# In the last expert slot, the loads of Q, K and V wait block by block for the stores that they read

## What is computed

```python
logits = xn @ sn - sigmoid(gates)            # 4096 x 16 experts
w = softmax over the active experts          # at least two of them
y = einsum('nc,ech->neh', x, p)              # p: q_proj, k_proj, v_proj
q, k, v = einsum('ne,neh->nh', w, y)         # each 4096 x 128
attn = softmax(q @ k.T / sqrt(128))          # all 4096 keys for all queries
o = attn @ v
out = einsum('enh,ehc->nc', w * o, o_proj)   # 16 experts back to 256 channels
return x + gb * out
```

## Time and profile before

| | us |
|---|---|
| median of 3 runs (1463.3 to 1464.61) | 1464.16 |
| profiled execution | 1462.89 |
| its span, first to last instruction | 1461.2 |
| PE busy | 1378.4 (94%) |
| DVE busy | 1157.5 (79%) |
| POOL busy | 710.0 (49%) |
| ACT busy | 672.8 (46%) |

### The profile page before, as it was taken

One profiled execution on the slowest core, in us unless ns is written; L12 is line 12 of the kernel. 1 busy time (PEld: TensorE's weight loads), 2 busy tenths in 40 slices (PEclk: granted clock), 3 DMA queues, 4 the chain that ended last, 5 costly groups with the idle time before them and its releaser, 6 DMA issues. The chain is left out here.

```text
span 1461.2 us, 20840 instructions
## 1 busy us (share of the span) xinstructions
PE 1378.4 (94%) x6884; PEld 1210.1 (83%) x6884; DVE 1157.5 (79%) x2192; ACT 672.8 (46%) x1331; POOL 710.0 (49%) x628
## 2 busy tenths in 40 slices
PE   5578999999999999999997989999999999999998
PEld 3458989999999999999997966878788787878776
DVE  5758586785876868767665888999999999989876
ACT  3340221302213022130011079888888888888983
POOL 3221131301313113121013167888889888988897
PEclk9688999999999999999999999999999999999999
DMA  4230110011100111000106450000000000000000
GB/s 135 72 97 15 31 38 27 26 39 31 38 27 26 38 31 38 27 26 24 52 25 209 148 192 15 8 23 21 15 30 15 30 16 29 15 22 16 15 15 30
DMA packets 84668, 63.24 MB, mean 43 GB/s; under 512 B 15520, under 2 KB 77392, under 8 KB 84304
## 3 DMA queue, kind: packets, MB, share of 16 engines
q1 hardware_dynamic: 56656, 46.69, 10.2%
q10 hardware_dynamic: 27904, 15.21, 3.5%
HBM read 36.72 MB, written 25.17 MB: 42 GB/s over the span
## 5 line engine op out<-in xcount | busy, mean ns | idle before, releaser
L1473 PE MATMUL ps<-w_hi,memory_r 128*128 128x384 f32 x2048 | 569.7, 343 | 5.8 <-DVE w_lo L886 3.0
L1246 DVE SCALAR_TENSOR_TENSOR wst<-ps,w_cur,wst 128x384 f32<-128x384 f32 x480 | 295.4, 615 | 171.1 <-PE ps L1473 157.8
L1473 PEld LDWEIGHTS ps<-w_hi,memory_r 128*128 128x128 f32 x2048 | 376.8, 189 | 10.0 <-DVE w_lo L886 3.1
L1690 POOL TENSOR_TENSOR memory_rest<-memory_rest,pf 128x512 f32<-128x512 f32 x248 | 346.4, 1397 | 67.0 <-ACT pf L1797 58.4
L1473 PE MATMUL ps<-w_lo,memory_r 128*128 128x384 f32 x1024 | 344.9, 337 | 0.0
L1863 DVE TENSOR_TENSOR p_lo<-pf,p_hi 128x512 fp32r<-128x512 f32 x256 | 282.4, 1103 | 34.3 <-ACT p_hi L1799 33.3
L1473 PEld LDWEIGHTS ps<-w_lo,memory_r 128*128 128x128 f32 x1024 | 194.3, 190 | 4.8 <-issue 1.4
L1797 ACT ACTIVATE pf<-ps 128x512 f32<-128x512 f32 x256 | 153.1, 598 | 71.7 <-PE ps L1969 54.7
L1757 ACT COPY ps<-shift_rows 128x512 f32<-128x512 f32 x254 | 151.7, 597 | 5.9
L1799 ACT ACTIVATE p_hi<-ps 128x512 fp32r<-128x512 f32 x256 | 152.0, 594 | 0.0
L1844 DVE TENSOR_REDUCE mx<-ps 128x1 f32<-128x512 f32 x224 | 147.7, 679 | 1.2 <-PE ps L1958 1.2
(11 more groups left out here) (216 smaller groups left out, 2105.0 us busy)
## 6 DMA issues: line engine op xcount, KB each, us to landing
qk_scratch<-wst ACTq DMA_DIRECT2D x56, 128.0 KB, 2.2
memory<-in_x SPq DMA_DIRECT2D x8, 512.0 KB, 4.0
x_scratch<-memory SPq DMA_DIRECT2D x8, 512.0 KB, 2.9
o_scratch<-memory_rest SPq DMA_DIRECT2D x16, 256.0 KB, 3.1
x2b<-x_scratch SPq DMA_DIRECT2D x32, 128.0 KB, 2.2
out_x<-memory_rest SPq DMA_DIRECT2D x32, 128.0 KB, 1.7
v_scratch<-wst ACTq DMA_DIRECT2D x60, 64.0 KB, 1.8
memory_r<-qk_scratch SPq DMA_DIRECT2D x9, 256.0 KB, 4.5
```

The lines of the kernel that those rows point to most:

```text
L1246: nc.vector.scalar_tensor_tensor(out=dst, in0=src, scalar=w, in1=dst, op0=ALU.mult, op1=ALU.add).then_inc(moe_acc, 1)
L1473: ins = nc.tensor.matmul(ps[:, s % MOE_BANKS, 0:H3], x_part[p][:, k, rows], w_part[:, k, e].rearrange("p t h -> p (t h)"), start=(k == 0 a ...
L1690: nc.gpsimd.tensor_tensor(p_sum[:, p], p_sum[:, p], pf[:, j % PB], ALU.add).then_inc(p_summed, 1)
```

## The change

The two waits for the stores of all 28 tiles of blocks 0 to 6 go. Ahead of the queries stands a wait for the stores of eight tiles, that is blocks 0 and 1. Ahead of each high key block g stands a wait for the Q and K stores of tiles up to the end of block g, and ahead of the low keys and values of block g one for the V stores up to there. No instruction is moved from its place in any queue, and the other engines' programs are the same.

```diff
                         sp.wait_ge(moe_mm, (NB - 1) * STEPS)
                         sp.wait_ge(u_ready, NB)
                         sp.wait_ge(bu_mm, NB)
-                        sp.wait_ge(qk_out, 32 * (NT - TT))
-                        sp.wait_ge(v_out, 32 * (NT - TT))
+                        sp.wait_ge(qk_out, 32 * 2 * TT)
 
                         def load_queries(n):
                             for l, q_part in enumerate((q_hi, q_lo)):
@@ -507,11 +506,13 @@
                         def load_high_keys(g0, g1):
                             for g in range(g0, g1):
                                 keys = slice(g * BT, (g + 1) * BT)
+                                sp.wait_ge(qk_out, 32 * (g + 1) * TT)
                                 sp.dma_start(k_hi[:, keys].bitcast(F32), qk_dram[0, :, 1, keys]).then_inc(k_in[g], 16)
 
                         def load_rest(g0, g1):
                             for g in range(g0, g1):
                                 keys = slice(g * BT, (g + 1) * BT)
+                                sp.wait_ge(v_out, 32 * (g + 1) * TT)
                                 sp.dma_start(k_lo[:, keys].bitcast(F32), qk_dram[1, :, 1, keys]).then_inc(kv_in[g], 16)
```

## The result

The changed kernel took 1452.29 us, the median of four runs (1451.81 to 1453.87), against 1464.38 us for the kernel before in the same comparison. The ratio is 0.9922, with a 95% interval of 0.991 to 0.9935. The profiled execution took 1451.81 us, 11.1 us less than that of before, and its span is shorter by 11.1 us too.

What follows compares the result with a forecast made beforehand. TensorE, 94% busy, was taken as the bound, with time to gain where it stalls or runs at a lower clock. Median 1464.16 less 10.63 us for the stall gave 1453.5 us; range 1451.8 to 1456.8.

Steps and rivals of the forecast that it cites:

- The wait that goes: SP queue, last expert slot: 11.3 + 1.2 us of waiting ahead of the first load goes; load issued at about 757.3.
- rival E: SP queue: another wait, hidden behind line 499, ends as late, so no gain: 1464.2 us, chance 0.02.
- The met waits: SP's added waits for stores long landed: 0.05 us each, 0.2 us for four among the first keys.
- The arrival of the keys: Key block 0 lands at 763.1, 3.3 us before PE needs it at 766.45 for the first maximum.
- The cost of the stall: PE at the first maximum in the last slot: 10.63 us lost, 9.06 waiting and about 1.57 lower clock and restart.
- The output chain: Output-part stores behind the loads: first group ends near 783, second starts at 787.9, an estimated 3 us late, covered; cost nothing.
- rival D: Output chain's second group makes ACT late beyond 13.1 us of cover; slower, 1471.2 us, chance 0.02.
- Rival C: VectorE can't catch up or the next block's waits fall otherwise: 1 to 3 us back, 1454.5 to 1456.5, chance 0.05.
- Rival B: First loads land twice as slowly; PE's stall shrinks to 1.6 us plus 1.57 of lower clock: 1456.7 us, chance 0.03.
- 0 to 1 us in either direction: Allowance for effects behind the slot and others not seen, priced at 0 to 1 us either way.

Runs made afterwards that it cites:

- `chain_last_b`: Changed kernel with low keys and values of blocks 3 to 6 issued ahead of the second group of output parts, run again: 1452.34 us (two runs).
- `late_by_5`: Changed kernel with SP's first load also waiting for the fifth step of slot 7: 1454.54 us, ratio 0.9934.
- `one_wait_again`: Changed kernel with the fourteen block waits replaced by two waits for all 28 tiles behind the first six loads, run once more: 1451.40 us, ratio 0.9912.

## Why the prediction was right

- **The wait that goes.** The first load was forecast for 757.3 and came at 757.14. No other wait stood behind line 499, so rival E was empty. The met waits cost even less than the 0.05 us allowed for each: the four issues of high keys with their four waits take 1.85 us, and took 1.86 without them.
- **The arrival of the keys.** 763.1 was forecast; the first load of `k_hi` was issued at 758.01 and took 4.5 us, so it landed at 762.5, 3.8 us before PE's need, not 3.3. The step took the landing from a place with output stores behind the loads. Block 0 took 3.6 to 4.5 us in the seven profiles in which it came early and alone, 3.9 to 5.3 in the four in which output stores followed the loads at once, and 5.5 and 5.6 in the two in which tile 27's stores were under way beside it.
- **The cost of the stall.** 10.63 us forecast, 10.68 measured in the stretch, of which 9.06 are the wait and 1.62 slower matmuls (1.57 forecast). In the rows the undisturbed piece takes 767.80 - 766.29 = 1.51 us, as the rows of before had it. By the Trainium skill's spacing of matmuls ("TensorE: Matmul & The Clock Gate", section "Wait — 56ns, not 53.3ns?") that piece was an estimated 1.41 us and the sum 10.74; the measured 1.51 speaks against it, but 10.68 lies midway between the two sums.
- **The output chain.** The first group ended at 781.8 (783 forecast), the third cast of ACT was at 774.77 ("near 774"), the second group's first store at 787.75 (787.9), and its two stores took 5.3 and 6.1 us to land (6.1). Two sizes were off, without effect: the first pair landed in 2.0 to 2.3 us, not 3.2, and so did, before the change, the second group's first pair, so that it became some 3.8 us slower and not 3. ACT's wait ahead of tile 29 shrank from 7.02 to 4.90 us, 2.1 us: its third cast had waited 2.65 us for POOL before, which hides a part. `chain_last_b` shows that the cover is real for 6.5 us more; that it is 13 us wide, as rival D had it, wasn't tried.
- **Rival C.** Nothing came back. PE's idle time in the stretch, other than the wait, is 1.07 us before and after, and behind the stretch the span is 0.27 us shorter, not longer.
- **Rival B** asked for slower loads; `late_by_5` brings about the same small stall by late ones. In its profiled execution 1.8 us came on top of a wait of 2.2, where B took 1.57 on top of 1.6. There the load takes 5.5 us against 4.5 and tile 27's stores 4.8 against 2.2. The rule of the Trainium skill that DMAs of SP and ACT share the 16 engines and interleave ("DMA: Bandwidth & Descriptors", section "Issuing engines are not separate DMA queues") agrees with this. The stores are the clearer sign, as the load took up to 5.3 us without tile 27's stores too.
- **The size.** The median moved by 12.1 us and not 10.6. The term that I set at "0 to 1 us in either direction" for unseen effects is the one that was too small: one and the same program took 1455.5 us in one series and 1451.4 in another. The change itself is worth 10.7 us by one profile of each kernel; the further 1.4 I take for scatter of the comparison, which comes to 11.7 in the second series. That isn't shown. The low end of the range, 1451.8, left this scatter hardly any room: the kernel of `one_wait_again`, with the same stretch, took 1451.40. That the median fell inside is in part luck.

What stays open is what sets PE's clock in the prologue and right behind the last slot, and why the four runs of one series were all slower.

## What to carry to other kernels

A wait for "all stores so far" costs what its last store costs, even where the reader needs only the oldest data; look for the first consumer, put its loads in front of that wait, and leave the rest as coarse as it is. If the wait can't be loosened, moving the first consumer behind the landing gives the same. An edit in one stage is best measured by the time between two instructions around that stage in the trace, as the medians of the whole moved by up to 4 us here with no change made.

## What was not expected of the hardware

TensorE's granted clock fell to about its lower level, 1.2 GHz (0.54 over 3.75 us), after a wait of only 2.23 us, and the price of 1.6 to 1.9 us was about the same for waits of 2.2 to 9.1 us. In that one execution a short stall in an otherwise full PE stretch cost nearly twice its length, 4.06 us. And the first 150 us, where the granted clock is 0.81 and PE busy for 104 of 151 us in the changed kernel, took 3 us more or less from one execution to another, while the medians of one and the same program lay 4 us apart (1455.5 and 1451.4); that the first is the main cause of the second is argued from the profiles, one for each series, and what follows the last slot adds up to 1.6 us of its own.
